# The first four tiles of a recurrent-attention and expert kernel on Trainium2: norms ahead of low parts, own banks for two tiles, weights converted by 128 outputs, and turns of the identity on an idle TensorE

## What is computed

```python
# block 1, on xn = layernorm(x)
r = sigmoid(xn @ Wr.T);  k = xn @ Wk.T;  v = xn @ Wv.T
scale = exp(pos * log(sigmoid(decay)))
state = cumsum(k * v / clip(scale), axis=time) * scale
out = groupnorm_over_sequence(r * state) * gn_weight + gn_bias
x = x + out @ Wo.T
# block 2, on layernorm(x): router over 64 experts, top 4, gated experts
# with up to 64 tokens each, and one shared gated expert
x = x + experts(layernorm(x)) + shared(layernorm(x))
```

## Time and profile before

| | |
|---|---|
| median of 3 runs | 696.03 us |
| the profiled execution | 696.56 us |
| its span | 694.7 us |
| busy: TensorE, VectorE, POOL, ScalarE | 95%, 46%, 32%, 23% |
| memory read, written | 179.48 MB, 24.13 MB |

### The profile page before, as it was taken

The page is one execution under the profiler, slowest core; times in us unless marked ns, Lnnn a source line. Parts: engine busy times, 40 slices in busy tenths (PEclk is TensorE's granted clock), DMA queues, the critical chain, the costliest instruction groups (busy, mean ns, idle before and its releaser), DMA issues. The chain is left out here.

```text
span 694.7 us, 8795 instructions
## 1 busy us (share of the span) xinstructions
PE 658.8 (95%) x3165; PEld 389.7 (56%) x3165; DVE 316.5 (46%) x750; ACT 162.8 (23%) x268; POOL 219.8 (32%) x210
## 2 busy tenths in 40 slices
PE   4999999999999898999999999999999999999982
PEld 2687878878878753444454454445444444444430
DVE  5887567849958682222233222323323323232321
ACT  5923114633211411211111111112112111111210
POOL 5537446535558222021221220203220122212112
PEclk9999999999999999999999999999999999999997
DMA  8201005722875988999999999999999999999973
GB/s 321 81 7 55 1 31 191 266 74 79 314 265 205 347 325 326 402 405 404 391 399 400 363 399 386 403 369 388 387 405 385 370 385 388 402 396 366 394 225 44
DMA packets 53628, 203.95 MB, mean 294 GB/s; under 512 B 7878, under 2 KB 8262, under 8 KB 53201
## 3 DMA queue, kind: packets, MB, share of 16 engines
q1 hardware_dynamic: 37504, 170.06, 61.3%
q0 software_dynamic: 9072, 21.52, 13.0%
q10 hardware_dynamic: 7008, 11.80, 4.5%
HBM read 179.48 MB, written 24.13 MB: 293 GB/s over the span
## 5 line engine op out<-in xcount | busy, mean ns | idle before, releaser
L657 POOL DMA_INDIRECT out_dram<-ym,midx x32 | 51.3, 1604 | 282.2 <-DVE ym L1266 130.4
L1613 PE MATMUL bank<-w_sb,xT 128*64 128x384 f32 x768 | 129.1, 489 | 0.8 <-ACT xT L884 0.8
L1398 PE MATMUL bank<-x_hi,w_parts 128*128 128x512 f32 x368 | 115.3, 396 | 2.2 <-DVE x_lo L997 2.2
L1613 PEld LDWEIGHTS bank<-w_sb,xT 128*64 128x64 f32 x768 | 53.0, 137 | 71.0 <-issue 67.8
L1398 PEld LDWEIGHTS bank<-x_hi,w_parts 128*128 128x128 f32 x368 | 70.0, 191 | 18.0 <-DVE x_lo L997 3.0
L1398 PE MATMUL bank<-x_lo,w_parts 128*128 128x512 f32 x184 | 71.0, 395 | 0.0
L1201 DVE TENSOR_TENSOR sg<-sg,bank 128x384 f32<-128x384 f32 x32 | 17.8, 555 | 116.6 <-PE bank L1613 62.6
L1531 PE MATMUL bank<-sh_sb,xS 128*128 128x384 f32 x208 | 69.2, 486 | 0.0
L1634 PE MATMUL bank<-w_sb,guT 128*64 128x512 f32 x288 | 65.9, 592 | 2.8 <-DVE ym L1266 2.8
L1531 PEld LDWEIGHTS bank<-sh_sb,xS 128*128 128x128 f32 x208 | 38.7, 191 | 24.1
L911 ACT ACTIVATE y<-bank,wcol 128x512 fp32r<-128x512 f32 x26 | 17.9, 687 | 121.3 <-PE bank L1634 121.3
(11 more groups left out here) (189 smaller groups left out, 939.1 us busy)
## 6 DMA issues: line engine op xcount, KB each, us to landing
w_sb<-in_L_ffn_w_down SPq DMA_DIRECT2D x48, 768.0 KB, 21.1
w_sb<-in_L_ffn_w_gate SPq DMA_DIRECT2D x48, 768.0 KB, 16.6
w_sb<-in_L_ffn_w_up SPq DMA_DIRECT2D x48, 768.0 KB, 19.5
extra<-in_L_ffn_w_gate SPq DMA_DIRECT2D x16, 768.0 KB, 20.1
extra<-in_L_ffn_w_up SPq DMA_DIRECT2D x16, 768.0 KB, 19.9
extra<-in_L_ffn_w_down SPq DMA_DIRECT2D x16, 768.0 KB, 22.7
ring<-in_L_attn_x SPq DMA_DIRECT2D x14, 256.0 KB, 3.7
xS<-xt_dram SPq DMA_DIRECT2D x13, 256.0 KB, 18.2
```

The lines of the kernel that those rows point to most:

```text
L657: pool.indirect_dma_start(out=out[:, :], out_offset=bass.IndirectOffsetOnAxis(ap=midx[j % 3][u][:, :], axis=0), in_=ym[u][:, :], in_offset ...
L1398: ins = pe.matmul(ps[u][:, :], w, xp, start=(n == 0), stop=(n == len(parts) - 1))
L1613: ins = pe.matmul(ps[e * C:(e + 1) * C, 0:I], xT[:, c, e * C:(e + 1) * C], gate_up(2 * j + u, e, k)[:, c, :], start=(c == 0), stop=(c == K ...
```

## The change

It has four parts, all before step 4.

- VectorE normalises tiles 0 to 3 before it makes any low part. Tiles 2 and 3 are written to two other buffers and turned into two other banks, those of k and v of step 1, so no turn of tiles 0 to 3 waits for a low part.
- Each of Wr, Wv, Wk is converted by chunks of 128 outputs, the chunk that one step uses: twelve conversions of 512 columns on ScalarE, and as many low parts as before, each now with the semaphore of its matrix. Steps 0 to 3 wait for the chunk they use.
- Step 0 takes hi*hi, then low weights, then low parts of x, and starts on the four high parts of x.
- TensorE turns the identity 14 times before the first tile, and 9, 8, 2 and 4 times behind tiles 0 to 3, into a bank that step 1 overwrites.

```diff
@@ PSUM banks and places of tiles 2 and 3
+        def outputs(i, c):
+            return raw[i][:, :, c * P:(c + 1) * P]
+        def x_bank(n):
+            return (ps_t[0], ps_t[1], ps_k[1], ps_v[1])[n] if n < 4 else ps_t[n % 2 if n < TILES else 1]
+        def xn_place(n):
+            return xw_ring[n - 2] if n in (2, 3) else xn[n % 2]
@@ POOL
-            for i in (0, 2):
-                for c in range(KC):
-                    if c == 0:
-                        pool.wait_ge(hi_ready, i + 1)
-                    ins = pool.tensor_tensor(w_lo[i][:, :, c, :], split(raw[i], c), w_hi[i][:, :, c, :].bitcast(F32), ALU.subtract)
-                ins.then_inc(lo_ready, 1)
+            def low(i, c):
+                pool.wait_ge(hi_ready[i], c + 1)
+                pool.tensor_tensor(w_lo[i][:, c, :, :], outputs(i, c), w_hi[i][:, c, :, :].bitcast(F32),
+                                   ALU.subtract).then_inc(lo_ready[i], 1)
+
+            low(0, 0)
+            low(0, 1)
+            low(2, 0)
+            low(2, 1)
+            for c in range(2, KC):
+                low(0, c)
+                low(2, c)
@@ ScalarE
-            def high(n):
-                act.wait_ge(raw_in[n], 16)
-                act.activation(w_hi[n], raw[n][:, :, :].rearrange("p k (c m) -> p c k m", m=P), ACT.Copy).then_inc(hi_ready, 1)
+            def high(i, c):
+                act.wait_ge(raw_in[i], 16)
+                act.activation(w_hi[i][:, c, :, :], outputs(i, c), ACT.Copy).then_inc(hi_ready[i], 1)
 
             turned_x(0)
+            high(0, 0)
             turned_x(1)
-            high(0)
             turned_x(2)
             turned_x(3)
-            high(1)
-            high(2)
+            high(1, 0)
+            high(0, 1)
+            high(2, 0)
+            high(1, 1)
+            high(2, 1)
+            for c in range(2, KC):
+                for i in range(3):
+                    high(i, c)
@@ VectorE
-                need(dve, xn_turned, n - 1)
-                normalise(xin_place(n)[0], xn[n % 2]).then_inc(xn_ready, 1)
+                if n >= 4:
+                    dve.wait_ge(xn_turned, n - 1)
+                normalise(xin_place(n)[0], xn_place(n)).then_inc(xn_ready, 1)
...
             for n in range(1, 4):
                 x_stats(n)
                 x_norm(n - 1)
-                if n == 1:
-                    dve.wait_ge(setup, 1)
-                    dve.tensor_scalar(dec[:, 2, :], dec[:, 1, :], 1e-7, None, ALU.max).then_inc(setup, 1)
-                else:
-                    x_low(n - 2)
-                if n == 3:
-                    x_norm(3)
-            x_low(2)
-            x_low(3)
-            dve.wait_ge(hi_ready, 2)
+            x_norm(3)
+            dve.wait_ge(setup, 1)
+            dve.tensor_scalar(dec[:, 2, :], dec[:, 1, :], 1e-7, None, ALU.max).then_inc(setup, 1)
+            for n in range(4):
+                x_low(n)
             for c in range(KC):
-                ins = dve.tensor_tensor(w_lo[1][:, :, c, :], split(raw[1], c), w_hi[1][:, :, c, :].bitcast(F32), ALU.subtract)
-            ins.then_inc(v_lo_ready, 1)
+                dve.wait_ge(hi_ready[1], c + 1)
+                dve.tensor_tensor(w_lo[1][:, c, :, :], outputs(1, c), w_hi[1][:, c, :, :].bitcast(F32),
+                                  ALU.subtract).then_inc(lo_ready[1], 1)
@@ TensorE
-                if s % STEPS in (0, KC):
+                if s == 0:
+                    pe.wait_ge(xhi_ready, TILES // 2)
+                elif s % STEPS in (0, KC):
                     pe.wait_ge(xlo_ready, s // STEPS * TILES + (h + 1) * TILES // 2)
...
-                    if s == 0:
-                        pe.wait_ge(hi_ready, i + 1)
+                    if s < KC:
+                        pe.wait_ge(hi_ready[i], s + 1)
+                    if 0 < s < KC:
+                        pe.wait_ge(lo_ready[i], s + 1)
...
-                        parts = parts[0::3] + parts[1::3] + parts[2::3]
+                        parts = parts[0::3] + parts[2::3] + parts[1::3]
                     for n, (w, xp) in enumerate(parts):
+                        if s == 0 and n == KC:
+                            pe.wait_ge(lo_ready[i], 1)
                         if s == 0 and n == 2 * KC:
-                            pe.wait_ge((lo_ready, v_lo_ready, lo_ready)[i], (1, 1, 2)[i])
+                            pe.wait_ge(xlo_ready, TILES // 2)
...
+            def keep_busy(count):
+                for _ in range(count):
+                    pe.transpose(ps_r[1][:, 0:P], ident[:, :], ident[:, :])
+
             pe.wait_ge(ident_steps, 2)
-            for n in range(4):
-                turn_x(n)
+            keep_busy(14)
+            turn_x(0)
+            keep_busy(9)
+            turn_x(1)
+            keep_busy(8)
+            turn_x(2)
+            keep_busy(2)
+            turn_x(3)
+            keep_busy(4)
```

More of the change, by code:

```diff
@@ L300, in moe_block @@
         power_ready, inv_made = sem("power_ready"), sem("inv_made")
-        hi_ready, lo_ready = sem("hi_ready"), sem("lo_ready")
-        v_lo_ready = sem("v_lo_ready")
+        hi_ready, lo_ready = ([sem(f"{n}_ready_{m}") for m in "rvk"] for n in ("hi", "lo"))
         wo_hi_ready, wo_lo_ready = sem("wo_hi_ready"), sem("wo_lo_ready")
@@ L697, in turned_x @@
             def turned_x(n):
-                bank_n = n % 2 if n < TILES else 1
                 act.wait_ge(xn_turned, n + 1)
@@ L701, in turned_x @@
                     act.wait_ge(k_ready, STEPS)
-                act.activation(tile_part(x_hi, n), ps_t[bank_n][:, :].rearrange("p (c t) -> p c t", c=KC),
+                act.activation(tile_part(x_hi, n), x_bank(n)[:, :].rearrange("p (c t) -> p c t", c=KC),
                                ACT.Copy).then_inc(xhi_ready, 1)
@@ L996, in x_low @@
                     dve.wait_ge(k_ready, STEPS)
-                dve.tensor_tensor(tile_part(x_lo, n), ps_t[bank_n][:, :].rearrange("p (c t) -> p c t", c=KC),
+                dve.tensor_tensor(tile_part(x_lo, n), x_bank(n)[:, :].rearrange("p (c t) -> p c t", c=KC),
                                   tile_part(x_hi, n).bitcast(F32), ALU.subtract).then_inc(xlo_ready, 1)
@@ L1336, in turn_x @@
                 pe.wait_ge(xn_ready, n + 1)
-                need(pe, xlo_ready, n - 1 if n < TILES else n)
-                bank_n = n % 2 if n < TILES else 1
+                if n >= 4:
+                    pe.wait_ge(xlo_ready, n - 1 if n < TILES else n)
                 for c in range(KC):
-                    ins = pe.transpose(ps_t[bank_n][:, c * P:(c + 1) * P], chunk(xn[n % 2][:, :], c), ident[:, :])
+                    ins = pe.transpose(x_bank(n)[:, c * P:(c + 1) * P], chunk(xn_place(n)[:, :], c), ident[:, :])
                 ins.then_inc(xn_turned, 1)
```

6 lines of the change are left out of this document (1 added, 5 removed).

## The result

The changed kernel takes 697.68 us in the median of 20 runs (696.81 to 698.74), the kernel before 695.67 us in 20 runs on the same chip: ratio 1.0025, 95% interval 1.0019 to 1.0032. By the ratio that is 1.75 us more, 1.3 to 2.2 by the interval; the medians themselves lie 2.0 us apart. The forecast was 0.85 us more, with 694.9 to 699.0 as the range: the side and the mechanism are right, the size is half of what was measured.

What follows compares the result with a forecast made beforehand. The bound was ScalarE's list at the front and the chain behind it, TensorE's start hidden: table load +1.5 us, less 0.7 us of slack, gave 0.85 us on the path; median 696.03 + 0.85 = 696.9 us, range 694.9 to 699.0.

Steps and rivals of the forecast that it cites:

- the chain from ScalarE's list to step 4: Front: ScalarE's conversions, exponentials and copy of v lead over POOL and VectorE to step 4, forecast at 61.0 for 60.16.
- kv of step 0: VectorE's product at the head of the chain: forecast to move from 33.01 to 33.85, +0.85 us.
- Norms ahead of low parts: VectorE before step 0: norm 3 at about 10.5 to 11.05 instead of from 11.58, its turn at 11.1.
- The identity turns: TensorE before step 0: 14 turns in idle time, 0.12 us apart once the clock is up, real turns held at most 0.2 us.
- The rival that it doesn't rise: TensorE's clock stays low during the turns, turn 3 ends at 14.8: +2.8 us, 698.8; late or missing rise 0.25.
- The rule of the Trainium skill named there: TensorE's full clock "doesn't engage" for transposes; by it the low-clock rival would be the forecast.
- The wait for wk: ScalarE idles 1.2 us before wk's first conversion, since wk lands at 14.42; the table load then comes +1.5 us later.
- the rival of the late clock: Low clock during the turns, +2.8 us, chance 0.25; decides only if turn 3 ends after 12.9, as ScalarE waits for wk until then.
- v of step 1: TensorE in step 1: idle from 31 to 32.9, waiting for ScalarE's copy of row_w.
- VectorE's inverse: Clipped inverse before kv of step 0: forecast 0.3 to 0.5 us earlier, worth nothing since ScalarE's copy of v is later.
- the shift stays to the end: Behind step 4 other engines and loads move alike, so the 0.85 us shift lasts to the kernel's end.
- the wait for the norm of tile 6: TensorE before the turn of tile 6: norm at about 41.5, step 1 through at 38.4; 2 to 3 us idle.

Runs made afterwards that it cites:

- step 0 later: Changed kernel with 20 instead of 4 identity turns between turn 3 and step 0: 699.23 us, ratio to before 1.0044.
- four conversions more: Changed kernel with four more ScalarE conversions of 512 columns behind the twelve, written where nobody reads: 700.06 us, ratio to before 1.0055.
- whole conversions: Changed kernel with the three matrices again converted whole, 2048 columns each, in the old places: 696.37 us, ratio to before 1.0000.
- the kernel before with twelve parts: Kernel before with only the twelve conversions of 512 columns and their low parts, none of the rest: 698.32 us, ratio 1.0036.
- runs with the shortened lists: Exponentials for positions 0 to 511 only, out_lo of step 0 earlier, Wo's low parts spread: changed kernel 695.43 us, kernel before 695.40 us; further runs moved norms.
- the change with halved exponentials: Changed kernel with eight exponentials of 512 instead of 1024 columns, out_lo of step 0 earlier, Wo's low parts spread: 695.43 us, ratio 0.9989.

## Why the prediction was right, and where it was off

**The bound.** It had the chain from ScalarE's list to step 4 as the limit, with TensorE's start hidden. With step 0 later, kv of step 0 and step 4 stayed; with four conversions more, both moved with a slope of one; with whole conversions the loss was gone. That ScalarE's conversions are the cause is shown.

**Norms ahead of low parts.** Norm 3 was put at 10.5 to 11.05 with 0.54 us. It began at 10.22 and took 1.49. The duration was the error: the change converts wr's first part early, and so POOL begins its low part at 10.15, beside this norm. With whole conversions the same norm took 0.55. The Trainium skill, SBUF — State Buffer, section SBUF: two separate sides, describes a pair of ports that GpSimd and some forms of VectorE's instructions (a 2-port mode, or two inputs from SBUF) share: whichever starts first has it for its whole instruction, and the other stands. By it the norm would stand until POOL's instruction ends at 11.42 and be through soon after; it ended at 11.71, and in the kernel before with twelve parts at 12.65 behind 12.37, so the traces agree, if the norm is of such a form, which no row shows. The prediction counted POOL's conversions at nothing and didn't ask what lay beside them. The turn of tile 3 was at 11.76 for 11.1.

**The identity turns.** The clock was up when the real turns came, as the forecast took it, with 0.11 for 0.12 us between turns; but in six of the seven later traces with these turns it rose only at 9.7 to 11.7. That it was up at 6.33 in the profiled execution is luck in that part. The rival that it doesn't rise had 0.25. The rule of the Trainium skill named there (TensorE: Matmul & The Clock Gate, section Part 4: PE-mode transpose), that the full clock does not engage for transposes, does not hold here: fourteen turns and nothing else ran before 6.33, and the next stood at half the spacing; in all eight traces with these turns the clock rose before any other matmul. The rival's price was right in kind: where the clock came late the identity turns held the real ones back, for 0.3 us at kv of step 0 between two traces of the change.

**ScalarE.** The wait for wk was to be 1.2 us and was 0.32, since x_hi of tile 3 came at 12.54 for 11.75. What norm 3 lost, the wait gave back. That is no luck: the rival of the late clock had it that until turn 3 ends at 12.9 ScalarE waits for wk anyway, and it ended at 12.51. A conversion was 0.52 for 0.50 us. The table load is at 19.33 for 19.05, and the copy of v at 32.01 + 0.59 = 32.60 for 32.36.

**POOL, VectorE, TensorE behind it.** POOL's v at 32.68 for 32.4, kv of step 0 at 34.07 for 33.85, v of step 1 at 33.24 with 0.55 us of wait before it (for 2 us: TensorE was later at this point, by the 0.9 us by which step 0 ended late, 21.5 for 20.6, and by 0.66 us of wait for the norm of tile 4, whose place behind slower exponents, 5.74 for 3.73 us, I had not followed), the turn of tile 6 at 41.73 for 41.5 with 2.29 us of wait, step 4 at 61.17 for 61.0. From the table load on, each landmark of the path is within 0.3 us; step 0 itself came at 13.19 for 12.4, where it costs nothing. VectorE's inverse, forecast 0.3 to 0.5 us earlier than before, came 0.3 later (31.34), still ahead of ScalarE's copy. In the front the sum is 1.06 for 0.85, and the 0.2 us are the nine conversions at 0.52 instead of 0.50.

**The total.** 0.85 was forecast, 1.75 measured (1.3 to 2.2 by the interval). The profiled pair differs by 1.22 us, 1.06 of it in the front. What can't be confirmed is the step "the shift stays to the end": in the profiled pair it nearly does (0.81 at the last gate matmul, 1.2 at the end of the span), but the ratio of all runs is 0.5 us above that pair. Among the traces the end moves by about 1 us with the wait of TensorE in the last group and with low-clock stretches of 3.4 us; neither trace of the pair has one before 684 us, so the pair can't show what they add. In the last group such a stretch stands in seven of the ten traces of kernels with the change, and in one of the four without it. Too few to show that the change brings it about, and I know no mechanism; 0.5 us of the difference stays open.

**What wasn't named.** The forecast priced the change as it stood and left it there. It named the wait for the norm of tile 6, but not what that wait would be worth. The runs with the shortened lists show that VectorE's list, not only ScalarE's, lay over TensorE's start.

## What to carry to other kernels

An earlier start of the busiest engine can be worth nothing until the lists that feed it are shorter as well. Here two covers lay over each other (ScalarE's exponentials and the norm of tile 6), and the same change cost 1.75 us with them and gave 2.0 us with both gone; the norm of tile 7 showed as a third, with 0.91 us of wait, but what its removal gives in time is not shown. Look at the first wait behind the place that you speed up, take that away in both versions, and compare again. And when an operation is made ready earlier, ask which engine then begins beside a neighbour that it did not meet before.

## What was unexpected of the hardware

- Turns of the identity alone raised TensorE's granted clock. The record of the rise came at 5.8 to 11.7 us in eight traces with the same fourteen turns from 2.1 or 2.5 us on, and at 17.8 to 20.5 in six without them; so the turns bring it forward, but the moment cannot be counted on. The stretch table gives 1.00 also before the record, with turns 0.22 us apart (0.11 after).
- A norm on VectorE (128x512) takes 0.54 us alone and 1.4 to 1.65 beside a subtraction or product of 512 columns on POOL, and ends 0.28 to 0.29 us behind it (11.71 behind 11.42); four exponent instructions of 512 columns took 4.61 us beside POOL's low parts, and four of 1024 columns 3.70 where POOL worked beside the first 1.2 us only (the kernel with four conversions more).
- After waits of 2.0 to 2.4 us before the turn of tile 6 in four traces (the change a second time, whole conversions, four conversions more, the change with halved exponentials), and of 2.5 to 4.0 us in the last group of eight, the granted clock fell for 3.4 us; in the last group twelve matmuls then took 4.20 to 4.49 us instead of 2.79. It did not fall behind 2.29 and 3.08 us in the first trace of the change, nor behind 2.78 us in that of the kernel before. So the length of the wait alone does not tell whether it falls.
